# Cross-attention and experts kernel: 64-row block-diagonal products for the cross maxima, narrower value tiles, another order of steps and 22 products of ones

## The reference

```python
q = _ln(latents, sa_ln_g, sa_ln_b)
x = latents + _mha(q, q, sa_in_w, sa_in_b, sa_out_w, sa_out_b)         # 16 heads of 8
qc = _ln(x, ca_q_ln_g, ca_q_ln_b)
kv = _ln(tokens, ca_kv_ln_g, ca_kv_ln_b)                               # the context
x = x + _mha(qc, kv, ca_in_w, ca_in_b, ca_out_w, ca_out_b)
...
logits = h @ rw.T + rb                                                 # h = _ln(x, moe_ln_g, moe_ln_b)
vals, idx = jax.lax.top_k(logits, 2)                                   # 2 of 8 experts
h1 = gelu(h @ fc1_w[e].T + fc1_b[e])                                   # 512 hidden features
mixed = sum of gate * (h1 @ fc2_w[e].T + fc2_b[e])
return x + mixed
```

## Time and profile before

| | |
|---|---|
| median of 3 runs | 313.35 us (310.02 to 323.27) |
| span of the profiled execution | 306.8 us |
| TensorE busy | 282.9 us (92%) |
| VectorE busy | 168.7 us (55%) |
| ScalarE busy | 165.5 us (54%) |
| GpSimd busy | 51.5 us (17%) |

### The profile page before, as it was taken

One profiled execution on the slowest core, in us unless ns is written; L12 is line 12 of the kernel. 1 busy time (PEld: TensorE's weight loads), 2 busy tenths in 40 slices (PEclk: granted clock), 3 DMA queues, 4 the chain that ended last, 5 costly groups with the idle time before them and its releaser, 6 DMA issues.

```text
span 306.8 us, 4812 instructions
## 1 busy us (share of the span) xinstructions
PE 282.9 (92%) x1736; PEld 175.0 (57%) x1736; DVE 168.7 (55%) x333; ACT 165.5 (54%) x221; POOL 51.5 (17%) x95
## 2 busy tenths in 40 slices
PE   7879399798999999998887999999999999999994
PEld 2436132343335324444335536669899989989984
DVE  3997688899889874867219665022425211211202
ACT  1542044687778889676741358774455453355060
POOL 2732983340220200023001220000100000000000
PEclk9985555999999999999996559999999999999999
DMA  7029412001000013000130000000000001000001
GB/s 241 7 56 426 169 38 71 1 16 52 3 2 2 4 30 76 3 5 5 28 78 2 4 2 2 2 0 2 0 4 0 0 2 34 2 0 2 0 0 36
DMA packets 7016, 10.82 MB, mean 35 GB/s; under 512 B 1429, under 2 KB 4945, under 8 KB 6737
## 3 DMA queue, kind: packets, MB, share of 16 engines
q1 hardware_dynamic: 6705, 10.08, 10.3%
q10 hardware_dynamic: 288, 0.43, 0.5%
HBM read 6.10 MB, written 0.52 MB: 22 GB/s over the span
## 4 chain that ended last, share of the span: by engine, by line
PE 75%; DVE 12%; DMA 4%; POOL 3%; issue 2%; ACT 2%; DVEq 0%; POOLq 0%
PE ps_r L952 19%; PE ps_o L884 10%; PE ps_r L864 9%; PE ps_r L937 5%; PE ps_r L939 5%; PE ps_r L938 5%; PE ps_r L822 5%; PE ps_x L745 3%; DVE row_max L652 3%; PE ps_o L896 3%; DVE row_max L656 3%; DMA hidden<-fc_w 3%; PE ps_o L891 3%; PE ps_r L834 2%; POOL fc_low L448 2%
## 5 line engine op out<-in xcount | busy, mean ns | idle before, releaser
L525 ACT ACTIVATE probs<-ps_r 128x1024 f32<-128x1024 f32 (+1 forms) x88 | 83.8, 985 | 30.5 <-PE ps_r L864 24.5
L652 DVE TENSOR_REDUCE row_max<-ps_r 128x2 f32<-128x1024 f32 x64 | 75.3, 1220 | 13.8 <-PE ps_r L822 12.8
L553 ACT ACTIVATE hidden<-ps_r,cols_sb 128x512 f32<-128x512 f32 x64 | 42.6, 688 | 43.9 <-PE ps_r L939 43.2
L952 PEld LDWEIGHTS ps_r<-fc_sb,hidden 128*128 128x128 f32 x512 | 59.7, 192 | 1.9 <-issue 0.5
L952 PE MATMUL ps_r<-fc_sb,hidden 128*128 128x128 f32 x512 | 60.4, 275 | 0.0
L721 DVE SCALAR_TENSOR_TENSOR x_sb<-ps_r,gate,x_sb 128x128 f32<-128x128 f32 x64 | 18.0, 344 | 62.2 <-PE ps_r L952 62.2
L822 PE MATMUL ps_r<-k_tile,q_tile 32*128 32x512 f32 x128 | 33.1, 558 | 4.6 <-DVE row_max L652 2.0
L884 PE MATMUL ps_o<-probs,v_aug 128*16 128x512 f32 x256 | 35.4, 625 | 0.0
L864 PE MATMUL ps_r<-q_tile,k_tile 32*128 32x512 f32 x128 | 31.5, 505 | 2.9 <-DVE row_max L652 1.4
L822 PEld LDWEIGHTS ps_r<-k_tile,q_tile 32*128 32x128 f32 x128 | 14.1, 217 | 23.7 <-issue 13.4
L656 DVE TENSOR_REDUCE row_max<-ps_r 128x4 f32<-128x616 f32 x32 | 23.7, 792 | 7.1 <-PE ps_r L834 6.9
(11 more groups left out here) (133 smaller groups left out, 322.7 us busy)
## 6 DMA issues: line engine op xcount, KB each, us to landing
q_tile<-q_part SPq DMA_DIRECT2D x36, 64.0 KB, 2.1
hidden<-fc_w SPq DMA_DIRECT2D x1, 2048.0 KB, 8.4
fc_sb<-fc_w SPq DMA_DIRECT2D x1, 2048.0 KB, 13.3
k_tile<-k_part SPq DMA_DIRECT2D x12, 64.0 KB, 2.1
x_sb<-x SPq DMA_DIRECT2D x2, 256.0 KB, 4.4
fc_sb<-w_rep SPq DMA_DIRECT2D x1, 512.0 KB, 5.2
q_tile<-max_rows SPq DMA_DIRECT2D x32, 8.0 KB
out<-x_sb SPq DMA_DIRECT2D x2, 256.0 KB, 2.3
```

The source lines that it names most:

```text
L525: nc.scalar.activation(probs[:, i:i + w], ps_r[:, slot("s", r), 0:w], ACT.Exp, scale=SCALE).then_inc(s_read, 1)
L553: ins = nc.scalar.activation(hidden[:, FC * (x_e % 2) + c], ps_r[:, slot("s", r), a], ACT.Gelu, bias=col(C_FC1_B + FC * (x_e % E) + c))
L652: nc.vector.tensor_reduce(heads[:, 2 * pair:2 * pair + 2, t], ps_r[:, slot("m", r)], AX.X, ALU.max).then_inc(m_read, 1)
L952: mm = nc.tensor.matmul(ps_r[:, slot("m", r), 0, t * D:t * D + D], hidden[:, FC * (n % 2) + c, t * P:t * P + P], fc2_sb[:, e, c], start=(c ...
```

## The change

1. **Cross maxima.** A new tile `kc_pairs` holds, for each two heads of 64 rows, their context keys block-diagonally in 308 columns. GpSimd clears it (2464 elements in a partition) and fills it with four more copies of 32 x 1232 in the step `kc_diag`. A cross `max` step now takes all four heads and one tile of 128 queries, in two matmuls of 64 rows and 308 columns, and waits for `pairs_ready` in place of `kc_moved`. VectorE still reduces 128 x 616 to 4 columns in a step.
2. **Narrower values.** `v_aug` has 9 columns for each head in place of 16, `vc_aug` 16 in place of 32. One clearing of `v_aug` is gone.
3. **`c_hat`** is gone: the context is normalised in place.
4. **The order** is another one, and holds ten `warm` words with 22 products of ones into `ps_x` (128 x 128 by 128 x 512, bf16), each word waiting until `ps_x` has been read. `fc1_split` is no longer in the experts' order.

```diff
 ORDER_OF_STEPS = """
-    ln:0 hat:0 hT:0 ln:1 ctx_ln:0 hat:1 qk0:0 ctx_hat:0 clear:0 qk0:1-3 hT:1 max:2 clear:1 max:4 load_fc:0
-    fc1_split:0-2 q:1 max:5-6 max:1 ctx_T:0 v:1 max:3 fc1_split:3 max:0 v:0 max:7 max:18 neg:0 max:21 max:16 mT:0
+    ln:0 hat:0 ln:1 ctx_ln:0 clear:1 warm:3 hT:0 hat:1 warm:1 qk0:0 qk0:2 max:2 hT:1 max:7 max:1 clear:3 warm:3 q:1
+    max:4 max:3 warm:1 v:0 max:6 max:5 warm:3 max:0 neg:0 v:1 max:16 qk0:1 max:22 mT:0 qk0:3 max:17 max:21 k:1
...
-        v_aug = sb("v_aug", [P, B, QT, H, 16])
-        vc_aug = sb("vc_aug", [P, B, H, 32])
+        kc_pairs = sb("kc_pairs", [P, B, G, 2 * T], F32R)
+        v_aug = sb("v_aug", [P, B, QT, H, DH + 1])
+        vc_aug = sb("vc_aug", [P, B, H, 16])
...
-                    sp.wait_ge(m_read, 4)
+                    sp.wait_ge(m_read, max(M_RING["qk0", g] for g in range(G)) + 1)
                     sp.dma_start(hidden[:, :, :], fc1_w).then_inc(fc1_loaded, 16)
...
+                    nc.gpsimd.memset(kc_pairs[:, :, :, :].bitcast(F32), 0.0).then_inc(pairs_cleared, 1)
...
+                        src = kc_tile[rows_j, :, :].bitcast(F32).rearrange("p g (b t) -> p b g t", b=B)
+                        nc.gpsimd.tensor_copy(kc_pairs[rows_j, :, :, j % 2 * T:j % 2 * T + T], src) \
+                            .then_inc(pairs_ready, 1)
...
-                        pe.wait_ge(kc_moved, 16 * G * len(K_PARTS))
+                        pe.wait_ge(pairs_ready, 4)
                         to = wait_for_slot("m", r)
-                        for i in range(2):
-                            for a in range(2):
-                                rows_j = slice(32 * (2 * pair + a), 32 * (2 * pair + a) + 32)
-                                mm = nc.tensor.matmul(ps_r[:, to, a, i * T:i * T + T],
-                                                      q_tile[rows_j, b, g, (t + i) * P:(t + i) * P + P],
-                                                      kc_tile[rows_j, g, b * T:b * T + T], start=True, stop=True,
-                                                      tile_position=(32 * (2 * pair + a), 0))
+                        for a in range(2):
+                            rows_a = slice(64 * a, 64 * a + 64)
+                            mm = nc.tensor.matmul(ps_r[:, to, a, 0:2 * T], q_tile[rows_a, b, g, t * P:t * P + P],
+                                                  kc_pairs[rows_a, b, g, :], start=True, stop=True,
+                                                  tile_position=(64 * a, 0))
...
-                            mm = nc.tensor.matmul(ps_o[32 * j:32 * j + 16, :], v_aug[:, b, c, 4 * g + j],
+                            mm = nc.tensor.matmul(ps_o[32 * j:32 * j + DH + 1, :], v_aug[:, b, c, 4 * g + j],
```

More of the change, by code:

```diff
@@ L75 @@
-    neg:15 mT:15 max:83 proj:2 neg:12 scores:81 scores:80 ln:4 max:90 scores:79 pv:43 max:88 hat:4 mT:12 scores:87
-    scores:86 pv:42 oc:13 max:91 max:89 neg:14 hT:4 scores:85 pv:47 rows_split:0 scores:76 router:0 scores:77 pv:46
-    oc:15 gates:0 mT:14 scores:78 fc1:0-1 oT:13 fc1:2 pv:40 gT:0 scores:84 scores:82 pv:41 fc2a:0 b2:0 fc2b:0 oc:12
-    scores:83 fc1:3 oT:15 pv:45 fc1:4 pv:44 oT:12 oc:14 fc2a:1 oT:14 fc1:5 fc2b:1 osT:3 fc1:6 fc2a:2 fc2b:2 proj:3
-    fc1:7 ln:5 hat:5 fc1:8-9 fc2a:3 hT:5 fc2b:3 fc1:10-11 fc2a:4 fc2b:4 rows_split:1 fc1:12 router:1 gates:1 fc1:13
@@ new lines @@
+    max:68-69 osT:1 max:76 max:70 neg:11 proj:1 scores:72 scores:70 neg:9 ln:3 mT:11 scores:71 mT:9 hat:3 scores:66
+    pv:37 scores:64 hT:3 pv:36 oc:10 q:3 scores:67-68 pv:32-33 oc:8 scores:69 oT:10 scores:73-74 fc1_split:1 pv:35
+    pv:34 oT:8 oc:9 scores:75 pv:38-39 oc:11 oT:9 oT:11 fc1_split:3 max:84-85 max:87 max:86 max:95 max:93 max:92
+    neg:13 max:94 neg:15 mT:13 max:83 osT:2 max:80 max:82 mT:15 max:81 proj:2 neg:12 ln:4 scores:81 scores:79-80
+    pv:43 mT:12 max:88 scores:85-86 hat:4 pv:42 max:90-91 oc:13 hT:4 scores:87 rows_split:0 pv:46 scores:76-77
@@ new lines @@
+    max:89 router:0 pv:47 oc:15 gates:0 fc1:0-2 neg:14 gT:0 fc1:3 fc2a:0 b2:0 fc2b:0 fc1:4 mT:14 fc2a:1 fc2b:1
+    scores:78 oT:13 fc1:5 pv:40 scores:83 scores:82 pv:41 fc1:6 oT:15 fc2a:2 oc:12 fc2b:2 fc1:7-8 scores:84 oT:12
+    fc1:9 fc2a:3 pv:45 fc2b:3 pv:44 oc:14 fc2a:4 fc2b:4 fc1:10-11 oT:14 fc1:12 osT:3 fc1:13 proj:3 ln:5 fc2a:5 hat:5
+    fc2b:5 fc1:14 hT:5 rows_split:1 fc1:15 router:1 fc2a:6 gates:1 fc2b:6 fc2a:7 gT:1 fc2b:7 fc1:16-17 b2:1 fc1:18
+    fc2a:8 fc1:19 fc2b:8 fc2a:9 fc2b:9 fc1:20-22 fc2a:10 fc1:23 fc2b:10 fc2a:11 fc2b:11 fc1:24-26 fc2a:12 fc2b:12
@@ L83 @@
+    fc1:27-28 fc2a:13 store:0 fc2b:13 fc1:29-30 fc2a:14 fc1:31 fc2b:14 fc2a:15 fc2b:15 store:1
 """
@@ L666, in _ @@
                     dve.wait_ge(misc_read, MISC_USE[step] + 1)
-                    if g == G - 1:
+                    if n == max(range(n - g, n - g + G), key=lambda u: ORDER["oT", u]):
                         dve.sem_inc(o_normed, 1)
```

69 lines of the change are left out of this document (31 added, 38 removed).

## The result

| | before | changed |
|---|---|---|
| median | 318.31 us (310.02 to 329.14, 4 runs) | 301.11 us (300.98 to 302.3, 4 runs) |
| span of the profiled execution | 306.8 us | 300.6 us |

The ratio is 0.9693, 95% interval 0.965 to 0.9736: faster. It compares, for each kernel, the runs within 1.5% of its fastest; the two medians alone would give 0.946. The forecast was 304.0 us. A run's time is its span plus 1.7 to 1.9 us, so the profiled execution took 302.3 us, and one of the kernel before with the traced span of 306.8 us took 308.5 us.

The account below looks back on a forecast made before the run. The start of the first `fc1` product was taken to set the end, delayed by the first stage's waits. Terms summed to 7.7 us: span 306.8 to 299.1 us, plus 4.9 us from span to time, 304.0 us; range 294 to 313.

Parts of the forecast that it names:

- Splits and load off the front: First stage: with quad 0's maxima first, the 26th self-maxima reduction ends at 52.7 us against 60.7, gaining 8.0 us (3.2 to 10.0).
- Full clock up to 160 us: TensorE from the start to 160 us: ones and closer quad 0 products keep full clock, which the 8.0 us gain supposes.
- The rival in which the clock falls in the first stage: First stage: the clock falls anyway, the gain shrinks by 7.3 us, giving 311.3 us; chance 0.17.
- Ones: First stage: 22 products of ones cost nothing beside VectorE's backlog of reductions; uncovered, up to 9.0 us.
- The rival of the ones' waits: At the ten words of ones: waits for `ps_x` and uncovered products cost 21.2 us, giving 325.2 us; chance 0.07.
- one of my signs of being wrong: In the changed profile: TensorE held by VectorE ahead of a product of ones would show the forecast wrong; no size given.
- Load behind: Behind the second quad's maxima: the 4 MB expert load may delay the third quad's DMAs, costing 1.0 us (0 to 7.5).
- Splits beside `hat:3`: Before batch 1's cross maxima: two GpSimd splits beside VectorE's `x_hat` cost 1.5 us (0 to 2.8).
- 64-row products: Cross maxima: TensorE's price, +0.21 to -0.1 us a step, hides behind reductions, so 0; 3.4 us where TensorE is full.
- Filling `kc_pairs`: GpSimd between `neg:3` and `neg:7`: four more copies, 1.6 to 13.7 us, hide behind reductions, so 0; -4 us at worst.
- Tail of the cross stage: End of the cross stage: `fc1:0` and `hT:4` come ahead of some maxima and a score pair, gaining 1.0 us (0 to 2).
- the second fall stays: From about 163 to 184 us: the half-clock stretch remains, since products from `q:3` to `hT:4` nearly keep their order.

Follow-up runs that it names:

- d3: The kernel before, order untouched, with 77 products of ones between its steps: 308.88 us, ratio 0.9962.
- d4: c3 with the splits of experts 1 and 3 back beside `hat:3`, ahead of batch 1's cross maxima: 300.0 us.
- b1: The kernel before with only the load of expert weights and the eight splits moved behind the front of its own list: 311.75 us.
- r0: The changed kernel itself, unedited, run six more times: 305.39 us, ratio to before 0.9633.
- a2: The changed kernel with the splits of experts 1 and 3 moved behind batch 1's cross maxima: 305.94 us.
- c2: The changed kernel up to `proj:2`, from there on the list of the kernel before: 310.51 us.
- a1: The changed kernel without its 22 products of ones: 307.04 us.
- c3: The changed kernel with the splits of experts 1 and 3 behind batch 1's cross maxima and 32 more products of ones: 297.28 us, ratio to before 0.9517.
- d2: c3 without its later ones, keeping the late splits and the six ones between the first scores: 295.76 us, ratio to before 0.9528.
- d1: c3 without `kc_pairs`, with 32-row products and the old widths of `v_aug` and `vc_aug`: 297.39 us.
- c1: The kernel before up to `proj:2`, from there on the changed kernel's list: 305.48 us, ratio to before 0.9764.

## Why the prediction came out

The number was right, 304.0 forecast and 301.1 us measured, and so was the sign, but luck had a part in it: errors of the sum cancelled. The lead of the first stage was lost in the middle, and the tail, costed at 1.0 us, won 5.9. And the step from span to time was mis-sized: the forecast's span was 299.1 us, 1.5 us below the measured 300.6, but I added 4.9 us for what lies around a span, where the runs show 1.7 to 1.9. The rest of the 4.9 was the spread of the kernel before, whose traced execution was one of its best, not a part of a run.

The time that is left has two parts, order and clock. Nearly full clock on both sides is the cleanest view: d3 (old order) and d4 (new order, splits in the changed kernel's places) both run at 0.98 to 0.99 in their profiles and have spans of 304.1 and 298.6 us, 5.5 us apart. From before (306.8) to d3 is 2.7 us, from the changed kernel (300.6) to d4 2.0 us. So the profiled pair's 6.2 us are 5.5 us of order and 0.7 us of clock, if the ones cost both kernels the same. They don't quite: from `q:3` to the 92nd reduction d3 takes 3.7 us more than the kernel before, d4 2.7 us more than the changed one, so about 1 us of the 5.5 may be the ones themselves. The front's ones, 49 in d3 and 28 in d4, are not separated at all. By medians the order makes 8.9 us (308.88 to 300.0), though d3's ten runs go down to a clock of 0.956; and from 314.0 to 301.4 us (the median of the changed kernel's ten) it is 12.6 us: the kernel before loses clock in all its runs, the changed one deeply in three of ten.

**Splits and load off the front, +8.0 us**: measured 6.9 in the profiled pair; at full clock the 26th reduction ends at 52.42 us, where I had worked out 52.7. The mechanism was half right. The splits and the load alone (b1) give 2.4 us; the rest of the order, with `ctx_T`, `v:1` and two of the four `qk0` steps behind quad 0's maxima, has to give the others. With the front at full clock on both sides (d3 57.91, d4 52.26 us) the new one is 5.7 us ahead. Where the clock stays at half from 41 to 60 us, 0.8 us or less of the lead is left (r0, a2, c2). A value step ahead, +1.0: inside that figure, not seen apart.

**Full clock up to 160 us**: wrong, and this is the first step that failed. The lead of 6.9 us shrank to 2.4 by the 80th reduction. Over the 84.64 us between the two events the clock was 0.94 in place of 1.00, so about 10 us were at half clock, which can cost up to 5 us; 4.5 were lost. "Behind it both lists hold about the same work" is true, but the work ran slower. The rival in which the clock falls in the first stage too came true in three of ten runs of the changed kernel: they took 309.3 to 313.1 us, around the rival's 311.3, and the one that was traced (r0) had the long low stretch.

**Ones, 0**: right as a price in this kernel, as far as is seen, and too low as a worth. The 22 bring the first exponential 3 to 4 us forward (a1), but don't secure the lead; six more between the first scores do. That ones are free is true only beside waits: between `q:3` and the 92nd reduction 20 of them cost 2.8 us (c3 beside d2) and 22 cost 3.7 us (d3 beside the kernel before). The rival of the ones' waits, and with it one of my signs of being wrong, showed in one of ten words: TensorE waited 1.6 us for VectorE at about 19 us, while VectorE itself was busy throughout; from 30 to 54 us TensorE's waits ahead of a product of ones are 0.3 us for ScalarE and 0.2 us for VectorE.

**Load behind, -1.0**: 0. From 55 to 80 us no wait of TensorE ends with a DMA that the profile shows, and the `q_part` DMAs, which no longer stand behind the load, take 2.1 us in place of 7.5. The rows, of TensorE's timeline with idle time, and of the DMA issues:

```profile
57.49 0.49 PE L866 MATMUL ps_r<-q_tile,k_tile 32*128 32x512 f32 x2 [0.18 <-DVE row_max L656]
...
68.56 0.49 PE L866 MATMUL ps_r<-q_tile,k_tile 32*128 32x512 f32 x2 [0.65 <-DVE row_max L656]
```

```profile
q_tile<-q_part SPq DMA_DIRECT2D x36, 64.0 KB, 2.1
hidden<-fc_w SPq DMA_DIRECT2D x1, 2048.0 KB, 7.7
fc_sb<-fc_w SPq DMA_DIRECT2D x1, 2048.0 KB, 13.7
```

**Splits beside `hat:3`, -1.5**: the right place, and nearly the right size. Against the kernel before, whose four `x_hat` took 2.1 us beside one addition (from 144.51 to 146.64 us, the first of them in the earlier trace rows), the 4.0 us are 1.9 us more; against no GpSimd work beside them (1.11 us) they are 2.9 us more. I had taken a middle between slipping in ahead and waiting out both. The far end of 2.8 us was reached: each of the four VectorE instructions ended with one of the four of GpSimd. From the 80th reduction to `q:3` the changed kernel lost 3.3 us; up to 1.7 us of that can be the low stretch at slice 20 (0.86 over 12.28 us, so 3.4 us at half).
The Trainium skill, page "SBUF — State Buffer", section "SBUF: two separate sides", has, for VectorE instructions in a 2-port mode or with two inputs from SBUF, an exclusive lock held for a whole instruction. The rows look like such a lock, though none tells the mode of `x_hat`; my reading of the rule ("at most 1.3 us if the lock is passed on") did not fit them: it is passed on, but GpSimd's next instruction was there each time, so four were waited out.

**64-row products, 0**: right; a step takes 0.06 us less, behind reductions of 0.8 us. By the rule on row groups in the Trainium skill ("TensorE: Matmul & The Clock Gate", "Part 3: Packing small matmuls — row/col tiling") TensorE would have lost 3.4 us; c3 and d1 are 0.1 us apart, so nothing of that reaches the end. **Filling `kc_pairs`, 0**: right; four copies of 1.2 us, 4.8 us between the bounds of 1.6 and 13.7, and d1 without them is no faster:

```profile
L436 POOL CAST kc_pairs<-kc_tile 32x1232 fp32r<-32x1232 f32 x4 | 4.8, 1212 | 0.0
```

**Narrower values, +0.2**: 0 (d1).

**Tail of the cross stage, +1.0**: the second step that failed, the other way. From the 92nd reduction to the first `fc1` activations it went from 20.3 to 14.4 us. At full clock the old list takes 14.4 us too (d3) and the new one 12.8 (d4): 1.6 us are order, near the forecast's upper end, and the other 4.3 us are clock, 0.62 against 0.81. I had written that the second fall stays; it came later and was shorter (from 160 us on, slice 23 alone, where slices 22 to 24 were low). Why is open: c1 shows that it goes with the new tail (0.81 there too), but from the 92nd reduction to the first `fc1` activations TensorE is busy without a gap in the kernel before and in the changed one, so the reason isn't there.

## What to carry to other kernels

Follow one count of events through both traces before you believe a total: a forecast can be right at the end and wrong at every stage. In a kernel whose clock falls, cost an order by where TensorE works at half clock, not by the mean, and compare traces of like clock: one trace of a kernel with such a spread can show a lead of 6.9 us or of 0.8. Products of ones beside waits cost nothing that shows here; elsewhere they cost their own time, and raise the mean clock for it. Six in the right gap (here between the first scores, while ScalarE and VectorE get going) steadied all 16 runs. And keep GpSimd's long instructions away from the few short VectorE ones on which everything waits, at their new place as well as at the old one.
